# Three f32r products for the way down of two networks, from a ring of rounded and remaining chunks

## The reference, cut to what matters

```python
# x: (4, 1024, 256) float32; out1 = layernorm(x + attention), g(.) = layernorm
h = jax.nn.elu(out1 @ W1 + b1)                 # network 1 (the encoder's own)
y = g(out1 + h @ W2 + b2)
x = x + ga * y
z = g(x) * (1 + cb) + sb
hidden = z @ V1 + c1                           # network 2
imag = w_imag * sin(theta + hidden * 0.1)
q = hidden + (cos(theta) * w_real + sin(theta) * w_imag) * imag * 0.1
x = x + gb * (relu(q) @ V2 + c2)
```

## Time and profile before

| | |
|---|---|
| three runs | 1788.21, 1790.55, 1791.43 us; median 1790.55 |
| profiled execution, its own time | 1788.67 us |
| its span, and mean granted clock of TensorE | 1786.9 us, 0.917 of full speed |
| PE, PEld, DVE, ACT, POOL busy over the span | 86%, 71%, 64%, 32%, 17% |
| `networks`, first `up` matmul to last `back_down` matmul | from 1362.22 to about 1781.4 us |

### The profile page before, as it was taken

One profiled execution on the slowest core, in us unless ns is written; L12 is line 12 of the kernel. 1 busy time (PEld: TensorE's weight loads), 2 busy tenths in 40 slices (PEclk: granted clock), 3 DMA queues, 4 the chain that ended last, 5 costly groups with the idle time before them and its releaser, 6 DMA issues. The chain is left out here.

```text
span 1786.9 us, 21261 instructions
## 1 busy us (share of the span) xinstructions
PE 1541.0 (86%) x7960; PEld 1270.6 (71%) x7960; DVE 1139.2 (64%) x1877; ACT 570.4 (32%) x817; POOL 311.6 (17%) x359
## 2 busy tenths in 40 slices
PE   7855343599999839999997899999995999999998
PEld 6532143599999836666663688888883888888887
DVE  5453499322222267778863887878774666698885
ACT  1013210133333212223222333333324544555452
POOL 2310000255555301221131500000000000000000
PEclk8766765699999969999998999999997999999999
DMA  5501491299999230121101300100004000000001
GB/s 188 213 1 48 133 332 66 59 295 293 296 297 291 45 118 24 36 67 40 36 24 47 106 16 22 35 24 24 12 12 156 25 23 13 1 1 24 19 17 36
DMA packets 127555, 157.06 MB, mean 88 GB/s; under 512 B 13937, under 2 KB 95977, under 8 KB 126449
## 3 DMA queue, kind: packets, MB, share of 16 engines
q1 hardware_dynamic: 115680, 138.12, 24.0%
q0 software_dynamic: 9216, 12.59, 3.4%
q10 hardware_dynamic: 2576, 5.26, 0.8%
HBM read 122.35 MB, written 33.60 MB: 87 GB/s over the span
## 5 line engine op out<-in xcount | busy, mean ns | idle before, releaser
L2227 PE MATMUL ff_down<-ff_w,ff_hid 128*128 128x256 f32 x1024 | 238.3, 379 | 0.0
L2227 PEld LDWEIGHTS ff_down<-ff_w,ff_hid 128*128 128x128 f32 x1024 | 193.4, 190 | 28.3
L1055 PE MATMUL h_ps<-xT,w 128*128 128x128 f32 x1536 | 194.0, 286 | 1.0 <-ACT xT L996 1.0
L1055 PEld LDWEIGHTS h_ps<-xT,w 128*128 128x128 f32 x1536 | 187.4, 199 | 1.6 <-issue 0.9
L1026 DVE TENSOR_TENSOR pre<-h_ps,b1T 128x1024 f32<-128x1024 f32 x48 | 58.8, 1224 | 177.4 <-PE h_ps L1055 177.4
L116 POOL TENSOR_TENSOR ff_rstd<-ff_var,minus_half 128x4 f32<-128x4 f32 x24 | 24.2, 1010 | 678.7 <-DVE ff_var L111 501.6
L2211 PE MATMUL ff_ring<-ff_rowsT_hi,ff_w_hi 128*128 128x512 f32 x256 | 121.3, 474 | 8.4 <-DVE ff_rowsT_lo L2005 5.6
L1090 PE MATMUL k_ring<-w_hi,hT_hi 128*128 128x512 f32 x256 | 118.5, 463 | 9.9 <-DVE hT_lo L1250 6.4
L1431 PE MATMUL k_acc<-wide_rows,hk 128*128 128x512 f32 x256 | 121.1, 605 | 4.4 <-ACT wide_rows L1375 4.4
L1090 PE MATMUL q_ring<-w_hi,hT_hi 128*128 128x512 f32 x256 | 109.7, 429 | 11.3 <-PEq L99 6.8
L1720 PE MATMUL q_out_ps<-kv_sums,wide_rows 128*128 128x256 f32 x512 | 115.6, 379 | 0.0
(11 more groups left out here) (360 smaller groups left out, 2979.1 us busy)
## 6 DMA issues: line engine op xcount, KB each, us to landing
w<-in_L_ffn_W_dram SPq DMA_DIRECT2D x48, 1024.0 KB, 5.8
w<-in_L_ffn_W_dram SPq DMA_DIRECT2D x48, 256.0 KB, 6.0
expert_sum_dram<-f_zero SPq DMA_DIRECT2D x8, 1024.0 KB, 14.4
b_rows<-in_L_ffn_b_dram SPq DMA_DIRECT2D x48, 128.0 KB, 8.4
x<-in_L_attn_x_dram SPq DMA_DIRECT2D x4, 1024.0 KB, 12.4
h_dram<-hg SPq DMA_DIRECT2D x8, 512.0 KB, 2.9
hk<-expert_sum_dram SPq DMA_DIRECT2D x8, 512.0 KB, 4.4
hT_hi<-expert_sum_dram SPq DMA_DIRECT2D x8, 512.0 KB, 5.3
```

Source lines behind the costliest of these rows:

```text
L1055: last = pe.matmul(h_ps[:, q % 2, s * KD + c, :], w1[:, q, s, k, c::KD], xT[:, q % 2, k, :], start=(k == 0), stop=(k == KD - 1))
L2227: last = pe.matmul(down[:, j // 2, j % 2, :], hid[:, n % 2, c, j * P:(j + 1) * P], w2[n // NG][:, c, :], start=(c == 0), stop=(c == CF - 1))
```

## The change

The way down becomes three f32r matmuls in place of one f32 matmul: rounded hidden by rounded weight, rounded hidden by the weight's remainder, the hidden's remainder by the rounded weight. For this

- ScalarE copies each finished chunk of `hid` to f32r (`high_part`, 128 copies of 128x512) and GpSimd subtracts the copy from the chunk (`low_part`, 128 of 128x512). `hid` is now a ring of 3 chunks, the two parts are rings of 5;
- `back_down(m)` takes one chunk for all four 128-row tiles, four chunks after its way up (`LAG`), into PSUM banks of which there are three (before two); the ring of chunks has five slots (before six);
- both results of an item (`result(n-1, 0)` and `(n-1, 1)`) are taken at c = 3 of the next item; before, one at c = 6 and one at c = 0;
- GpSimd adds to x (`add_to_x` at c = 4 and 5) and adds the gated b2 (`shift_x` at c = 6); VectorE keeps the product with the gate (`gate_down`);
- the second weights are split too: SyncE loads them into `raw`, one after the other with the first weights, ScalarE rounds (`weights2_high`), VectorE subtracts (`weights2_low`), at m = 2 and 3, and m = 25 and 27; the other first weight at m = 9 and 11.

The core of the diff:

```diff
-RINGS = 6
-HALVES = 2 * G
+RINGS, BANKS = 5, 3
+LAG, PARTS, WHOLES = 4, 5, 3
...
-                sp.dma_start(w2[0][:], a["L1_attn_W2"].rearrange("(c p) n -> p c n", p=P)).then_inc(w2_in[0], 16)
...
                 sp.wait_ge(low_done, 1)
+                sp.dma_start(raw2, a["L1_attn_W2"].rearrange("(c p) n -> p c n", p=P)).then_inc(raw_in, 16)
+                load(2)
+                sp.wait_ge(low2_done, 1)
                 sp.dma_start(raw[:], a["L1_ffn_W1"].rearrange("(k p) n -> p k n", p=P)).then_inc(raw_in, 16)
...
+                def high_part(m):
+                    if m < W:
+                        act.wait_ge(ring_free, chunk_use(m) + 1)
+                    else:
+                        act.wait_ge(hid_ready, m - W + 1)
+                    if m >= PARTS:
+                        act.wait_ge(down_done, PAIRS * (m - PARTS + 1))
+                    act.activation(hid_hi[:, m % PARTS, :], hid[:, m % WHOLES, :], ACT.Copy).then_inc(part_high, 1)
...
+                        if 1 <= m <= W:
+                            high_part(m - 1)
+                        if m >= W + 2:
+                            high_part(m - 2)
...
+                def low_part(m):
+                    pool.wait_ge(part_high, m + 1)
+                    if m >= PARTS:
+                        pool.wait_ge(down_done, PAIRS * (m - PARTS + 1))
+                    pool.tensor_tensor(hid_lo[:, m % PARTS, :], hid[:, m % WHOLES, :], hid_hi[:, m % PARTS, :].bitcast(F32),
+                                       ALU.subtract).then_inc(part_low, 1)
...
                 def hid_free(m):
-                    if m >= 2 * CF and m % CF == 0:
-                        dve.wait_ge(down_done, PAIRS * (m // CF - 1))
+                    if m >= WHOLES:
+                        dve.wait_ge(part_low, m - WHOLES + 1)
...
+                def back_down(m):
+                    n, c = m // CF, m % CF
+                    high, low = w2[n // NG]
+                    pe.wait_ge(part_low, m + 1)
+                    for j in range(G):
+                        if c == 0 and j % 2 == 0 and PAIRS * n + j // 2 >= BANKS:
+                            pe.wait_ge(down_free, PAIRS * n + j // 2 - BANKS + 1)
+                        into, tile = bank(n, j // 2)[:, j % 2, :], slice(j * P, (j + 1) * P)
+                        pe.matmul(into, hid_hi[:, m % PARTS, tile], high[:, c, :], start=(c == 0 and j % 2 == 0), stop=False)
+                        pe.matmul(into, hid_hi[:, m % PARTS, tile], low[:, c, :], start=False, stop=False)
+                        last = pe.matmul(into, hid_lo[:, m % PARTS, tile], high[:, c, :], start=False, stop=(c == CF - 1 and j % 2 == 1))
+                        if j % 2:
+                            last.then_inc(down_done, 1)
...
+                    if m == LAG:
+                        pe.wait_ge(low2_done, 1)
```

More of the change, by code:

```diff
@@ L1957, in _ @@
                             turned_high(n + 1)
[L1958 to L1961, removed]
+                sin(ITEMS * CF - 1)
+                high_part(ITEMS * CF - 2)
+                high_part(ITEMS * CF - 1)
             @block.gpsimd
@@ L1983, in _ @@
+                for p in range(PAIRS):
+                    add_to_x(ITEMS - 1, p)
             @block.vector
@@ new lines, in _ @@
+                        if c == TURN_AT + (not is_elu(n)) and n + 1 < ITEMS:
+                            turned_low(n + 1)
+                        if c == 0 and 1 <= n and n + 1 < ITEMS:
+                            row_stats(n + 1)
+                        if c == 2 and 1 <= n and n + 1 < ITEMS:
+                            row_shift(n + 1)
+                        if n == 0 and c == 1:
+                            row_vectors()
+                        if c == 1 and is_elu(n):
+                            base_gain(n)
@@ L2186, in _ @@
+                        if c == 2 and is_elu(n):
+                            base_offset(n)
+                        if c == 3 and n:
+                            for p in range(PAIRS):
+                                result(n - 1, p)
+                        if c == 5 and 1 <= n <= NG:
+                            finish(n - 1)
+                    if n == 0:
                         wave_start()
+                add_wave(ITEMS * CF - 1)
+                bias_relu(ITEMS * CF - 1)
+                for p in range(PAIRS):
+                    result(ITEMS - 1, p)
@@ L2214, in up @@
                     last.then_inc(full, 1)
-                def back_down(n, h):
-                    j, half = h // 2, h % 2
-                    if j % 2 == 0 and half == 0:
-                        pe.wait_ge(down_free, PAIRS * n + j // 2 + 1)
-                    chunk = n * CF + (half + 1) * CF // 2 - 1
-                    if is_elu(n):
-                        pe.wait_ge(ring_free, chunk_use(chunk) + 1)
-                    else:
-                        pe.wait_ge(hid_ready, chunk - W + 1)
-                    for c in range(half * CF // 2, (half + 1) * CF // 2):
-                        last = pe.matmul(down[:, j // 2, j % 2, :], hid[:, n % 2, c, j * P:(j + 1) * P], w2[n // NG][:, c, :],
-                                         start=(c == 0), stop=(c == CF - 1))
-                    if j % 2 == 1 and half == 1:
-                        last.then_inc(down_done, 1)
+                def back_down(m):
[11 more added lines that the diff above has]
+                            last.then_inc(down_done, 1)
```

164 lines of the change are left out of this document (88 added, 76 removed).

## The result

The changed kernel takes **1797.01 us** (median of 6 runs, 1795.4 to 1798.61) where the kernel before takes 1790.83 beside it (6 runs, 1788.21 to 1791.56): ratio 1.0036, 95% interval 1.0023 to 1.0049, so slower by 6 us. The forecast was 1775, with 1767 to 1784 for its own case and 1752 to 1802 over all cases, and "faster" with a chance of 0.74. The profiled execution took 1796.55, its span 1794.7, at a mean granted clock of 0.91.

What follows compares the result with a forecast made beforehand. TensorE's stream was taken as the bound. Terms -35.3 + 11.7 + 4 + 1.5 + 2 + 0.7 = -15.4 took 1788.7 to 1773.3; the runs' median lies 1.9 us above: 1775, own range 1767 to 1784, all cases 1752 to 1802.

Steps and rivals of the forecast that it cites:

- 6, end: Behind the last matmul, the final addition to x goes from VectorE (0.69 us) to GpSimd (1.3 us): +0.7 us.
- Term 1: TensorE's way down: 1024 f32 records removed (221.2 us), 1536 f32r matmuls at 0.121 us added (185.9): -35.3 us.
- second: Rival: f32r matmuls of the way down run at the weight loads' pitch of 0.108 us, total 1759; chance 0.12.
- fourth: Rival: f32r matmuls of the way down cost more when every load counts, 0.130 us each, total 1786; chance 0.11.
- fifth rivals: Rival: f32r saves no passes at this width, 0.216 us per matmul, +110 us; chance 0.02.
- the first: Rival: `bias_relu` goes first and GpSimd waits, so the lock's stalls are gone, total 1763; chance 0.21.
- Term 3: Wave items: `bias_relu` waits out GpSimd's remainder; TensorE stalls 0.8 us at the bank, 0.75 at the turn: +11.7 us.
- the +1.5: `finish` of item 7 falls in a wave item that has no room: +1.5 us.
- "nothing" for remainders: Way down: remainders queued behind GpSimd's long instructions come 1 us late, but 2.4 us of slack take it; no cost.
- Term 4: Weights prepared mid-stage: at chunks 11 and 27 VectorE's subtraction delays freeing the bank, 1.7 us each and more: +4 us.
- Term 5: Stage start: first way down near 1378, 9 us lost against 10.2 before; some 4 us at half pace: +2 us.
- third rival: VectorE becomes the bound of the wave items, a whole remainder before every `bias_relu`: +15.5 us, total 1806; chance 0.17.

Runs made afterwards that it cites:

- experiment 2: Changed kernel with GpSimd's remainders, `shift_x` and `add_to_x` all cut short in network 2's (wave) items, output incomplete: 1776.04 us, ratio 0.9925 to the kernel before.
- experiment 1: Changed kernel with only GpSimd's remainders cut to 8 of 512 columns in the wave items, output not the reference's: 1792.52 us, ratio 1.001 to the kernel before.
- after: The changed kernel itself, without any follow-up edit: 1797.01 us, ratio 1.0036 to the kernel before.
- experiment 9: Changed kernel with one wait more: in wave items GpSimd's remainder of a chunk waits until VectorE ended the next chunk's `bias_relu`; 1807.01 us, ratio 1.0095.
- experiment 11: Experiment 10 with GpSimd's `row_power` moved ahead of the waiting remainder of chunk 7 and `shift_x` at chunk 1 instead of 6: 1772.91 us, ratio 0.9896.
- experiment 10: Changed kernel with the later remainder of experiment 9, two weight subtractions one chunk later and `finish(7)` one chunk later: 1791.92 us, ratio 1.0007.
- best version: The kernel of experiment 11: 1772.91 us, ratio 0.9896 to the kernel before.
- experiment 4: Changed kernel with `turned_low` put between `add_wave` and `bias_relu` at chunk 6 and `turned_high` ahead of the rounding copy: 1804.97 us, ratio 1.0073.

## Why the prediction was wrong, by its steps

The profiled spans differ by +7.8 us, the sum said -15.4. By the table (waiting is what an item takes over 23.44):

| step | forecast | measured |
|---|---|---|
| 1, the stream | -35.3 | 1536 x 0.120 - 221.2 = -36.9 |
| 3, lock, and `finish` | +11.7 and +1.5 | item 8 6.5, item 9 4.3, five of 2.1, "last" 5.4: +26.7 |
| 4, weights | +4 | 6.5 + 4.5 = +11.0 |
| 5, start | +2 | +5.2 |
| 6, end | +0.7 | 6.71 - 5.52 = +1.2 |

For "last" the undisturbed length is 28.3: an item without its transposes and four chunks more of the way down (23.44 - 0.9 + 5.8), near the 28.58 of experiment 2. The sum is +7.2, of the stage's 8.0.

**Term 1 was right** to 1.6 us, and so the second, fourth and fifth rivals were out (the first is out by `bias_relu`, which did not go ahead of the remainder): the 109 ns of the Trainium skill ("TensorE: Matmul & The Clock Gate", back-to-back issue gap) would be 0.011 us less than each start measured.

**Term 3 named the right mechanism and, with `finish`, priced it at half: 13.2 us for 26.7.** In many chunks `bias_relu` did start 0.2 us behind the remainder and took some 1.36 (its mean of 1.03 has chunks without one), and TensorE waited at the two places named. The 13.5 us that were missing are these:

- *The five items 10 to 14, 2.7 us.* The bank waited 1.10 us over the pitch and the turn 0.80, where the sum had 0.8 and 0.75. What failed is "VectorE has that second free in most chunks", used as if each chunk began afresh. From the `bias_relu` at 1700.50, ahead of the turned rows, the timeline shows VectorE without an idle moment to the results at 1717.02: three of 1.36, 1.51 and 1.13, `row_stats`, then 0.49, 1.03 and 0.96. Its 24.00 us in 26.00 leave no place to work lateness off (in experiment 1 the bank was late although the remainder just ahead of it took 0.20).
- *`finish` in item 8, 3.5 us there and 2.8 in item 9.* The step that failed is the +1.5: TensorE waited 5.61 us for the turned rows behind `finish`, and 5.51 us at half clock came after it. Experiment 2 leaves 3.34 of that wait, with no half clock behind. In after the first four instructions of `finish` took 2.69 us beside a remainder (1.67 in experiment 2), and VectorE waited 0.90 us for the power ahead of them (0.17).
- *The last item, 4.6 us.* The step that failed is "nothing" for remainders queued behind GpSimd's long instructions, on 2.4 us of slack. That slack is made of the way up, and the last item's way down runs out of it: TensorE waited 3.9 us for remainders, which the prediction itself named as a sign of being wrong.

The additions to x were cost at nothing as holders of `bias_relu`; experiment 1 shows that they hold it as well. The Trainium skill's line on who locks whom ("SBUF — State Buffer", who interferes with whom) agrees: the instructions that read PSUM and at most one tile stayed at 0.67 to 0.75 beside GpSimd throughout.

**Term 4 was mis-sized for three reasons.** VectorE came later in its row: its elu instruction ended at 1407.71, 0.46 us behind the bank's date, where the sum had it 1.35 ahead. The subtraction took 2.76, not 2.29, since it too began inside a remainder of GpSimd (in an elu item, where the sum had the lock at nothing); and the forecast stopped at the wait. Waits of 3.98 and 2.92 us were followed by 5.5 and 3.4 us at clock 0.50, half of which is lost: 3.98 + 2.8 and 2.92 + 1.7 give nearly the 6.5 and 4.5 of the two items. Only the start had a term for the clock.

**Term 5**: the first way down came at 1380.63, inside the 1378 to 1382 named, but 2.6 us behind the "near 1378" the sum used; VectorE had `row_vectors`, `base_gain` and `base_offset` ahead of the subtraction. With the window of 5.2 us at half clock, item 0 loses 14.2 us (31.81 less 17.6 of work); items 0 and 1 before lost 7.4 + 1.6, not 10.2.

The third rival, VectorE as the bound of the wave items, had the sign, but +15.5 us where 6 were measured, and TensorE busy under 9 tenths where 24.42 of 26.00 were. VectorE was nearly full (24.00 of 26.00); experiment 2 shows that what filled it was the waiting.

What stays open: how the 5.61 us in item 8 divide between `finish` and lock beyond what experiment 2 shows; why a wait is followed by half clock in one item and not in another; and 0.8 us of the stage, most of which is within the rounding of 0.120 (by whole items the stream gained 16 x 2.23 = 35.7, not 36.9).

## What to carry to other kernels

When a trace shows instructions of a full engine waiting out those of a helper, ask not only how much the helper does but which instruction of the other starts just behind it, and carry the delay forward chunk by chunk to the next date somebody waits for. A wait added to one instruction is paid by all that is queued behind it: experiment 9 lost 10 us by a good wait, and experiment 11 won 19 against experiment 10, which had that wait too, by moving two instructions out from behind it. Look also at the end of the stream, where the slack that hid a queue is gone: the last item here paid 3.9 us for it. And price a wait of TensorE of some us with the slow stretch behind it.

## What the runs showed of the hardware that was not expected

- A VectorE instruction of 4 columns took 2.06 us (0.17 otherwise) because GpSimd's of 2.40 had started 0.38 ahead; one of 0.49 (`bias_relu`) ended 0.3 us after GpSimd's, whatever that one's length (1.29 or 2.40).
- In network 2's items the lock costs GpSimd little: `add_to_x` takes 1.38 on average in after and 1.30 in the best version, `shift_x` 2.56 and 2.40. In network 1's items it is GpSimd that waits: a remainder took 3.31 us (1408.21 to 1411.52) beside the subtraction that VectorE had in its line from 1407.63 to 1410.39, and ended 1.13 behind it.
- The same wait of 2.1 us was followed by half clock in three items of experiment 4 and not in the next two.
